# In twelve attention slots the side keys' probabilities are turned by VectorE's block transposes instead of TensorE's second chunk

## The reference

```python
# attention: 16 heads of 32; a query sees the context rows at a distance of at most 64
scores = einsum('bhqd,bhkd->bhqk', qh, kh) / sqrt(32)
scores = where(abs(i - j) > 64, -inf, scores)
y = softmax(scores) @ vh                       # keys and values are both the context
x = x + y @ W_proj.T + b_proj                  # queries: layer norm of x
# feed-forward: a gated recurrence over the 8 sequences, state c of 512 x 512
ft = sigmoid(xt @ wf.T + c @ uf.T + bf);  it = sigmoid(xt @ wi.T + c @ ui.T + bi)
gt = tanh(xt @ wc.T + c @ uc.T + bc);     c = ft * c + it * gt
x = x + tanh(x_ln @ wo.T + c_final @ uo.T + bo)  # xt, x_ln: layer norm of the new x
```

## Time and profile before

| | |
|---|---|
| median of three runs | 939.13 us |
| the profiled execution's own time | 940.45 us |
| its span | 938.5 us |
| PE (TensorE) busy | 920.8 us, 98% |
| PEld (weight loads) busy | 716.7 us, 76% |
| DVE (VectorE) busy | 673.8 us, 72% |
| ACT (ScalarE) busy | 476.1 us, 51% |
| POOL (GpSimd) busy | 206.1 us, 22% |
| HBM traffic | 130 GB/s over the span |

### The profile page before, as it was taken

The page is one execution under the profiler, slowest core; times in us unless marked ns, Lnnn a source line. Parts: engine busy times, 40 slices in busy tenths (PEclk is TensorE's granted clock), DMA queues, the critical chain, the costliest instruction groups (busy, mean ns, idle before and its releaser), DMA issues.

```text
span 938.5 us, 21983 instructions
## 1 busy us (share of the span) xinstructions
PE 920.8 (98%) x7842; PEld 716.7 (76%) x7842; DVE 673.8 (72%) x2275; ACT 476.1 (51%) x1430; POOL 206.1 (22%) x236
## 2 busy tenths in 40 slices
PE   8999899999999999999999999999999999999998
PEld 5555567678877788887877888788877888888887
DVE  6888898888779977997799878987798531143222
ACT  6888666655555544554465555555655421131222
POOL 4575322211110111111111111111101100003444
PEclk9999999999999999999999999999999999999999
DMA  9564223224443543444544444434333150049862
GB/s 299 167 191 154 86 80 109 73 82 130 132 130 116 133 131 94 139 111 126 129 141 116 117 114 123 114 108 110 98 98 92 50 164 0 1 175 383 317 235 101
DMA packets 139348, 123.58 MB, mean 132 GB/s; under 512 B 46824, under 2 KB 104168, under 8 KB 137704
## 3 DMA queue, kind: packets, MB, share of 16 engines
q1 hardware_dynamic: 138520, 121.91, 42.7%
q10 hardware_dynamic: 720, 0.27, 0.2%
HBM read 87.70 MB, written 34.46 MB: 130 GB/s over the span
## 4 chain that ended last, share of the span: by engine, by line
PE 87%; DVE 6%; issue 3%; ACT 2%; DMA 1%; POOL 0%; SPq 0%; DVEq 0%; POOLq 0%; ACTq 0%
PE ps_g L699 18%; PE ps_g L701 17%; PE ps_g L700 17%; PE ps_a L746 5%; PE ps_a L768 5%; PE ps_m L699 3%; PE ps_v L789 3%; PE ps_m L701 3%; PE ps_m L700 3%; PE ps_m L821 2%; PE ps_a L701 2%; PE ps_a L700 2%; PE ps_a L699 2%; DVE probs L1028 2%; PE ps_v L794 2%
## 5 line engine op out<-in xcount | busy, mean ns | idle before, releaser
L916 ACT ACTIVATE probs<-probs,rowmin 128x192 f32<-128x192 f32 (+1 forms) x512 | 239.4, 470 | 114.2 <-DVE rowmin L1028 114.2
L1028 DVE CUSTOM_DVE_ANT_0 probs<-ps_a,mask 128x192 f32<-128x192 f32 (+1 forms) x512 | 166.0, 385 | 30.2 <-PE ps_a L746 29.4
L699 PE MATMUL ps_g<-state_hi,gate_w 128*128 128x512 f32 x336 | 133.6, 398 | 0.0
L701 PE MATMUL ps_g<-state_hi,gate_w 128*128 128x512 f32 x336 | 131.1, 390 | 0.0
L700 PE MATMUL ps_g<-state_lo,gate_w 128*128 128x512 f32 x336 | 130.9, 389 | 0.0
L1063 DVE STREAM_TRANSPOSE keys<-probs 32x128 f32<-32x128 f32 x420 | 125.6, 299 | 5.6 <-issue 0.3
L963 ACT ACTIVATE gate<-ps_g,bias 128x512 f32<-128x512 f32 x84 | 57.6, 686 | 105.4 <-PE ps_g L701 104.8
L916 ACT ACTIVATION_READ_ACCUMULATOR probs<-probs,rowmin 128x1 f32 x512 | 96.3, 188 | 0.0
L678 POOL TENSOR_TENSOR attn_lo<-recip,attn_hi 128x512 fp32r<-128x512 f32 x23 | 29.7, 1293 | 276.4 <-ACT attn_hi L929 276.4
L921 ACT ACTIVATE probs_t<-ps_a 128x512 f32<-128x512 f32 x108 | 59.3, 595 | 50.9 <-PE ps_a L768 50.9
L699 PE MATMUL ps_g<-x2t_even,gate_w 128*128 128x512 f32 x192 | 80.0, 417 | 0.0
(11 more groups left out here) (220 smaller groups left out, 1724.9 us busy)
## 6 DMA issues: line engine op xcount, KB each, us to landing
values<-ctx_rows SPq DMA_DIRECT2D x34, 256.0 KB, 4.4
xr<-x SPq DMA_DIRECT2D x32, 256.0 KB, 3.5
keys<-ctx_t SPq DMA_DIRECT2D x16, 512.0 KB, 4.3
x_dram<-xr SPq DMA_DIRECT2D x32, 256.0 KB, 2.4
gate_w<-x2t_dram SPq DMA_DIRECT2D x8, 1024.0 KB, 9.7
keys<-ctx_t SPq DMA_DIRECT2D x16, 384.0 KB, 3.5
x2t_dram<-x2t_even SPq DMA_DIRECT2D x12, 512.0 KB, 4.1
x2t_dram<-x2t_odd SPq DMA_DIRECT2D x12, 512.0 KB, 4.4
```

The source lines that it names most:

```text
L699: pe.matmul(ps, lhs[0], rhs[0], start=start, stop=False)
L701: return pe.matmul(ps, lhs[1], rhs[0], start=False, stop=stop)
L916: act.activation(row, row, ACT.Exp, bias=rowmin[:, i % 2, h:h + 1], scale=-1.0, accum_out=rowsum[:, i // G % 2, i % G, h:h + 1]).then_inc( ...
L1028: dve.tensor_tensor_reduce(probs[:, i % 2, h, 0:SEEN[t]], ps_a[h][:, score_at[i]:score_at[i] + SEEN[t]], mask[:, MASK0[t]:MASK0[t] + SEEN[ ...
```

## The change

Slots 0 to 3 (tile 0), 12 to 15 (tile 3) and 16 to 19 (tile 4) now take the second way of turning: those below slot 20 whose tile sees 192 keys. Slots 4 to 11 keep the two chunks. For these twelve slots TensorE turns the own 128 keys alone, still into ps_g[0]; VectorE's copy is gone and three block transposes are added, one slot earlier (step sides n+1 in slot n; sides 0 ahead of slot 0). At slots 0, 12 and 16 VectorE clears the one 32x32 block per head that lies in the queries' half but outside the window. The second part of the value product runs over the 64 side keys and the 64 queries that see them. The side keys' values are loaded to the partitions where these keys lie. Waits on turned_2 and cleared are counted anew.

```diff
+    def by_blocks(i):
+        return i >= OWN_BANKS or SEEN[i // G % TT] < KEYS
+
     def v_loads(i):
-        if G * i >= OWN_BANKS:
+        if by_blocks(G * i):
             return 1 + (i % TT > 0) + (i % TT < TT - 1)
         return 2
...
-    steps += [("score", 0), ("ln1", 1), ("score", 1), ("exp", 0), ("recip", 0)]
+    steps += [("score", 0), ("ln1", 1), ("score", 1), ("exp", 0), ("recip", 0), ("sides", 0)]
...
-            if n + 1 >= OWN_BANKS:
+            if by_blocks(n + 1):
                 steps.append(("sides", n + 1))
...
(SP, load_v: each test of G * i against OWN_BANKS becomes by_blocks(G * i))
...
(TensorE, turn)
-                        for c in range(2):
+                        for c in range(2 if not by_blocks(i) else 0):
...
-                        continue
-                    if i >= FIRST_TWO:
+                        if not by_blocks(i):
+                            continue
+                    elif i >= FIRST_TWO:
                         pe.wait_ge(masked, HPG * (i - i % 2 + 2))
...
(TensorE, value)
-                    if i < OWN_BANKS:
+                    if not by_blocks(i):
...
                     side = SIDE_Q[tile % TT]
+                    keys_of = SIDE_Q[tile % TT] if i < OWN_BANKS else slice(0, P)
...
-                                       values[:, tile % 2, 1, d], side_home[i][:, h, side],
+                                       values[keys_of, tile % 2, 1, d], side_home[i][keys_of, h, side],
...
(VectorE, score)
-                    if i - 2 >= OWN_BANKS:
+                    if i >= 2 and by_blocks(i - 2):
                         dve.wait_ge(turned_b, i - 1)
...
(VectorE, turn and sides)
-                if kind == "turn" and i < OWN_BANKS:
+                if kind == "turn" and not by_blocks(i):
                     some = min(SEEN[i // G % TT] - P, P)
-                    dve.wait_ge(turned_2, i + 1)
+                    dve.wait_ge(turned_2, sum(not by_blocks(n) for n in range(i + 1)))
...
+                    if i < OWN_BANKS and i % G == 0:
+                        t = i // G % TT
+                        empty, q = (BLK * (P // BLK - 1), WINDOW) if t == 0 else (0, BLK)
+                        dve.memset(side_home[i][empty:empty + BLK, :, q:q + BLK], 0.0).then_inc(cleared, 1)
+                        dve.wait_ge(cleared, sum(by_blocks(n) for n in range(0, i + 1, G)))
                     if i == OWN_BANKS:
                         dve.memset(side_home[i], 0.0).then_inc(cleared, 1)
-                        dve.wait_ge(cleared, 1)
+                        dve.wait_ge(cleared, sum(by_blocks(n) for n in range(0, i + 1, G)))
```

More of the change, by code:

```diff
@@ L520, in _ @@
                     need(sp, valued, G * (i - 1))
-                    own = P * t if G * i >= OWN_BANKS else KEY0[t]
+                    own = P * t if by_blocks(G * i) else KEY0[t]
                     sp.dma_start(values[:, i % 2, 0], ctx_rows[b, own:own + P, :]).then_inc(v_in[i % 2], DMA)
-                    if G * i < OWN_BANKS:
+                    if not by_blocks(G * i):
                         sp.dma_start(values[0:SEEN[t] - P, i % 2, 1], ctx_rows[b, own + P:own + SEEN[t], :])\
                           .then_inc(v_in[i % 2], DMA)
-                    if G * i >= OWN_BANKS and t > 0:
+                    if by_blocks(G * i) and t > 0:
                         sp.dma_start(values[0:WINDOW, i % 2, 1], ctx_rows[b, own - WINDOW:own, :])\
                           .then_inc(v_in[i % 2], DMA)
-                    if G * i >= OWN_BANKS and t < TT - 1:
+                    if by_blocks(G * i) and t < TT - 1:
                         sp.dma_start(values[WINDOW:P, i % 2, 1], ctx_rows[b, own + P:own + P + WINDOW, :])\
@@ L1053, in _ @@
                     dve.wait_ge(valued, i - i % 2 if i >= FIRST_TWO else i)
+                    if i < OWN_BANKS and i % G == 0:
[3 more added lines that the diff above has]
+                        dve.wait_ge(cleared, sum(by_blocks(n) for n in range(0, i + 1, G)))
                     if i == OWN_BANKS:
                         dve.memset(side_home[i], 0.0).then_inc(cleared, 1)
-                        dve.wait_ge(cleared, 1)
+                        dve.wait_ge(cleared, sum(by_blocks(n) for n in range(0, i + 1, G)))
                     if i == FIRST_TWO:
                         dve.memset(sides_t, 0.0).then_inc(cleared, 1)
-                        dve.wait_ge(cleared, 2)
+                        dve.wait_ge(cleared, sum(by_blocks(n) for n in range(0, OWN_BANKS + 1, G)) + 1)
                     for queries_of, keys_of, col in SIDES[i // G % TT]:
```

## The result

The changed kernel takes 950.32 us (median of 4 runs, 949.43 to 951.45) against 940.17 (4 runs, 938.74 to 941.36): a ratio of 1.011, 95% interval 1.0096 to 1.0123, so 9.0 to 11.6 us slower. I had forecast 945.0 with a range to 948.3: the direction was right and the size was not. The profiled execution took 949.94 us, its span 948.0, 9.5 more than before.

A forecast was written before the change was run, and what follows sets the result against it. VectorE's work between a projection's end and the next mult was taken to bound the changed stretch; 1.4 + 1.13 + 2.25 + 1.12 = 5.9 us made the profiled 940.45 into 946.35, forecast as 945.0 for the median, range 941.7 to 948.3.

The forecast's parts named there:

- tile 0: Slots 0 to 3: sides 1 delays ln1b and the clearing of c0_cols, so ScalarE and projection 0 start 1.4 us later.
- sides 12 ahead of mult 2: Slot 11: sides 12 with its memset delays mult 2 by 1.13 us; the copy it replaces was free beneath the projection.
- tile 3 behind its projection, with sides 16: From projection 2 on: value wait, sides 13 to 15 and 16, less three copies and the L1012 gain; +2.25 us.
- tile 4: Slots 16 to 19: the same as tile 3 without sides of the next tile; 2.25 - 1.13 = +1.12 us.
- value wait: Slots 12 and 16: sides n+1 must wait for value n behind the projection, starting 0.60 us later each time.
- The memset: Slots 0, 12 and 16: clearing 32x128 on VectorE, taken as 0.20 us with its wait.
- the free copies under the projections: VectorE's copy beneath a projection, as in slot 11, was off the path, so removing it saves nothing.
- ln1b's 0.35 us out of GpSimd's way: L1012 (ln1b) in tiles 3 and 4, started later, runs clear of a GpSimd instruction: 0.35 us saved, taken off twice.
- A: Rival: TensorE bounds tiles 3 and 4, so its saved work leaves the path, 3.6 us in all; 935.5 us, chance 0.06.
- B: Rival: slack absorbs the value wait and prologue, and the L1012 gain doubles; 2.6 us slower, 941.7 us, chance 0.14.
- C: Rival: sides waiting for values couples both engines in slots 13, 14, 17 and 18; 2.4 us more, 947.4 us, chance 0.14.
- D: Rival: the change does not do what it says, a slot falls back on the two chunks; 939.1 us, chance 0.02.

The follow-up runs named there:

- keep2: Changed kernel plus unread identity transposes in TensorE's idle places, nine places in tile 0 and others in tiles 3 and 4; 947.07 us, ratio 1.0076 to before.
- fill4: Changed kernel plus four unread identity transposes on TensorE behind the turn in each of the twelve slots; 948.88 us, ratio 1.0093 to before.
- keep: Changed kernel plus unread identity transposes in TensorE's idle places, three places in tile 0 and others in tiles 3 and 4; 949.41 us, ratio 1.0096 to before.
- gap: Kernel before plus one VectorE memset of 128x1536 ahead of each of mult 2 and mult 3, TensorE's work untouched; 945.81 us, ratio 1.0058 to before.
- swap_keep: As keep, but the next sides step stands behind ln1b instead of ahead of it in slots 0, 12 and 16; 947.57 us, ratio 1.0082 to before.
- tile3_only: Kernel before with only slots 12 to 15 turned by VectorE's blocks, tiles 0 and 4 left as before; ratio 1.0045 to before, 4.2 us.

## Why the prediction was wrong

**The step that failed** is in the first part: the clock was 1.00 also where TensorE is busy 8.1 of 10, "so gaps of this size cost no clock". The row showed only that the clock had survived that stretch, 110 to 120 us, and my own change made other gaps, next to waits for mult that grew from about 0.2 us to 1.44 and 1.55. I had worked out that VectorE would be late by over a microsecond ahead of two projections, and didn't ask what an idle TensorE does to its clock. No term, no rival and no bound had the clock in it, so the range ended short of the result. The runs put 3.0 us on it in the changed kernel's tile 4 (24.95 against 21.93), and the medians of changed and keep2 3.2 in all (ratios 1.0110 and 1.0076).

**The sum at full clock** was 5.9; keep2 has 7.1 by its ratio and 7.14 at projection 4, counted from the norm. By itself that miss of 1.2 us would have stayed in the range. By terms:

| term | forecast | measured | from |
|---|---|---|---|
| tile 0 | 1.4 | 1.82 and 2.06 | norm to projection 0, keep2 and fill4 |
| sides 12 ahead of mult 2 | 1.13 | 1.24 to 1.25 | interval 1 to 2, changed and keep2 |
| tile 3 behind its projection, with sides 16 | 2.25 | 2.57 | interval 2 to 3, keep and keep2 |
| tile 4 | 1.12 | 1.51 | interval 3 to 4, keep, keep2, fill4 |
| value wait, in the last two | 2 x 0.60 | 0.60 and 0.59 | projection to sides in keep2, to ln1b before |

The memset (0.165 and its wait), the free copies under the projections and ln1b's 0.35 us out of GpSimd's way (0.39 and 0.40 measured) came out as written. Too small was what a sides step takes from start to start. In tile 0 it is 1.58 us from the reciprocal through sides 0 to the next score, where the copy's slot took 0.79: +0.79 for my 0.43; sides 1 added 1.09 for 0.93. In tile 3 sides 16 with its memset took 1.35 for 1.13, which is most of the missing 0.32. In tile 4 the three sides steps took 0.98, 0.98 and 0.97 for 0.93 each, and the reciprocal and the turn2 product next to them 0.10 more each.

There is also a path through TensorE that I had overlooked. Its query L727 waited 1.32 us, not for ln1b (over at 67.84) but for resid L1088, which reads the same bank ps_m and ends at 68.44. The chain of waits of the changed kernel goes that way (start, length, what):

```profile
67.83 0.61 DVE xr L1088
68.44 0.14 issue
68.58 0.64 PE ps_m L727 x4
69.25 0.61 ACT queries L910
69.85 0.14 issue
69.99 2.02 PE ps_m L809 x8
```

In the kernel before, resid was over (64.57) ahead of the query (65.05), and TensorE had not to wait. At full clock this path costs nothing that can be seen, since VectorE is just as late by its own work, as its waits in keep2 show. It matters once the clock is low: in the changed kernel's tile 4 VectorE waited 0.43 us for row 17 (its columns, at 94.45) and about 0.3 us each at two later places, where the same steps of keep2 didn't wait. So the low clock of row 17 reached projection 4 by this way.

**The rivals.** A (TensorE's saving counts) fell: the four transposes and the smaller value product left no trace in any interval. B fell: the value wait and the prologue's term were there in full, and little was absorbed behind 97 us. C fell at full clock, where VectorE never waited in slots 13, 14, 17 and 18 for the products that it names; only with the low clock did a wait of that kind appear, 0.43 us. D fell: the copy L1054 (before L1049) is at x8, and the transposes in blocks went from x72 to x108. One count of mine was misread: of L758's 160 transposes 64 are left, and the 48 for the own keys moved to the line of the second way, L772; 112 is the two together.

**Beyond one profile.** The kernel before loses the clock in some executions too: of 17 timed beside the first experiments, the two of 941.62 and 943.26 us had a mean clock of 0.998, the others 0.999 or 1.0. Of the ten counted beside gap, four at 0.998 took 941.35 to 941.90 us and six at 1.000 took 938.93 to 939.73. So its margin is small, and the times of one kernel spread by the clock too; the changed kernel had 0.989 to 0.993 in all four executions.

## What to carry to other kernels

Where the engine that waits is TensorE, price a longer wait twice: the wait, and the work behind it at half the clock; a clock of 1.00 in a trace is that schedule's, not a licence for another. Find the steps that lie beneath a long product and leave the exchange work there, since the same transposes cost about 7.1 us ahead of the products and 2.2 in the place of the copies, counted at projection 4 with a full clock. Before two traces are subtracted, look whether they agree ahead of the first changed step; here they differed by 0.87 us. And a step that is late delays whoever shares a bank with it: follow the buffer, not only the data.

## What the runs showed of the hardware

A TensorE with the same instructions fell to the 1.2 GHz level after single waits of 1.78 and 1.75 us (gap), with projection 3.67 us long at the one level and 5.37 at the other, since the clock was full again before its end. In these projections the fall came at the start (81.4 us in the changed kernel, projection 3 at 81.43) or up to 0.9 us into the product (60.5 in gap, projection 2 at 59.97; 81.0, projection 3 at 80.18; 105.5 in swap_keep, projection 4 at 104.57). The length of one wait doesn't decide it: the kernel before has a wait of 1.53 us without a fall, and behind the same wait of 1.44 us projection 2 took 5.37 us in fill4 and 3.67 in the changed kernel and in tile3_only. What does decide it is open. Transposes of the identity, 9 of them in 1.20 us in the idle place, kept projections 2 and 3 at 2.4 GHz in the profiled executions of keep, swap_keep and keep2. And the first products of an execution can be slow where the windows read a clock of 1.00: the first 16 records of L746 took 0.94 us before the change, the same in the changed kernel (L749) 0.58; what the clock was there the profile doesn't show.
